# Relation masks made in memory under the attentions, negated scores, weights relative to the first head, ten row buffers

## The reference, cut to what matters

```python
sub, obj = rel_pair_index[:, 0], rel_pair_index[:, 1]          # 10000 pairs, below 1500
att = (q[sub] * k[obj]).sum(-1) / sqrt(64)                     # for each of 8 heads
scores = zeros((8, n, n)).at[:, sub, obj].set(att)
scores = where(adj == 0, -inf, scores)
scores[:, i, i] = 1e-7
out = x + (softmax(scores, axis=2).sum(axis=0) / 8) @ h
```

## Time and profile before

| | |
|---|---|
| median of 3 runs | 4285.27 us (4284.05 to 4287.05) |
| span of the profiled execution | 4283.1 us, 2.2 below the median |
| VectorE busy | 3536.2 us, 83% |
| TensorE busy | 3570.2 us, 83% |
| ScalarE busy | 2616.4 us, 61% |
| POOL busy | 1413.4 us, 33% |
| granted clock of TensorE, mean | 0.912 |

### The profile page before, as it was taken

How to read it: one execution, slowest core, us unless ns; L and a number is a source line. 1 busy time by engine, 2 the same in 40 slices (tenths; PEclk the granted TensorE clock), 3 DMA queues, 4 the chain that set the end, 5 groups by cost and what they waited for, 6 DMA issues and landing times. The chain is left out here.

```text
span 4283.1 us, 55860 instructions
## 1 busy us (share of the span) xinstructions
PE 3570.2 (83%) x20136; PEld 2068.0 (48%) x20136; DVE 3536.2 (83%) x5848; ACT 2616.4 (61%) x3072; POOL 1413.4 (33%) x1417
## 2 busy tenths in 40 slices
PE   6889989879888838687887889899997967788887
PEld 3689989534344414333343344577773422333333
DVE  4699999679999996799999925799984169999996
ACT  3677777559888875588897823454543344444442
POOL 0343200017778794399988811000001100000000
PEclk9999999989998969899898899999998988888888
DMA  4611100211110100511101034000002111111110
GB/s 151 246 32 27 32 27 22 84 46 50 43 45 23 37 17 23 170 40 42 30 20 42 18 125 151 22 19 19 19 9 74 69 64 59 44 49 45 45 44 15
DMA packets 160244, 228.80 MB, mean 53 GB/s; under 512 B 85137, under 2 KB 96288, under 8 KB 154672
## 3 DMA queue, kind: packets, MB, share of 16 engines
q1 hardware_dynamic: 148592, 191.33, 13.8%
q0 software_dynamic: 11376, 33.76, 2.2%
HBM read 158.48 MB, written 66.47 MB: 53 GB/s over the span
## 5 line engine op out<-in xcount | busy, mean ns | idle before, releaser
L1695 DVE SCALAR_TENSOR_TENSOR junk<-expd,mid 128x2048 bf16<-128x2048 f32 x440 | 1036.4, 2356 | 13.8
L579 ACT ACTIVATE steepz<-s1b,thr_h 128x1024 bf16<-128x1024 f32 (+1 forms) x832 | 733.5, 942 | 394.1 <-DVE mask L646 380.9
L732 PE MATMUL acc<-V,mask 128*128 128x198 bf16 (+1 forms) x5504 | 745.8, 274 | 100.4 <-DVE mask L646 51.5
L1595 ACT ACTIVATE junk_s<-expd,nmid 128x2048 bf16<-128x2048 f32 x264 | 528.8, 2003 | 129.6 <-POOL nmid L1655 116.1
L732 PEld LDWEIGHTS acc<-V,mask 128*128 128x128 bf16 x5504 | 478.7, 99 | 163.7 <-DVE mask L646 56.5
L1598 ACT ACTIVATE junk_s<-expd,nmid 128x2048 bf16<-128x2048 f32 x264 | 528.0, 2000 | 0.0
L2140 PE MATMUL psS<-KT,qs 64*128 64x512 f32 x1024 | 367.5, 728 | 130.7 <-DVE m L2253 125.5
L646 DVE TENSOR_TENSOR mask<-steepz,adjT 128x1024 bf16<-128x1024 bf16 (+1 forms) x832 | 438.4, 565 | 18.5 <-ACT steepz L579 8.6
L739 PE MATMUL acc<-V,adjT 128*128 128x99 bf16 (+1 forms) x5504 | 452.5, 220 | 0.0
L739 PEld LDWEIGHTS acc<-V,adjT 128*128 128x128 bf16 x5504 | 368.7, 99 | 49.6 <-issue 1.0
L1467 PE MATMUL psX<-parts,block 128*128 128x512 bf16 x1536 | 364.6, 394 | 10.4 <-DMA block<-adj_dram 10.4
(11 more groups left out here) (306 smaller groups left out, 5941.0 us busy)
## 6 DMA issues: line engine op xcount, KB each, us to landing
rows<-in_adj_dram SPq DMA_DIRECT2D x32, 1024.0 KB, 5.3
s1b<-sT_dram SPq DMA_DIRECT2D x32, 512.0 KB, 3.8
block<-adj_dram SPq DMA_DIRECT2D x32, 512.0 KB, 4.5
adj_dram<-adjT POOLq DMA_DIRECT2D x4, 2048.0 KB, 20.8
rel_table<-zeros POOLq DMA_DIRECT2D x64, 128.0 KB, 19.9
y_dram<-yo SPq DMA_DIRECT2D x32, 256.0 KB, 2.0
step_dram<-xo SPq DMA_DIRECT2D x32, 256.0 KB, 2.0
A<-step_dram SPq DMA_DIRECT2D x8, 1024.0 KB, 13.6
```

What stands on the lines that cost most here:

```text
L579: act.activation(steepz[:, m % RELUS, :], s1b[:, q % 4, :], ACT.Relu, bias=thr_h[:, u, 1, j:j + 1], scale=STEEP).then_inc(relu_ready, 1)
L732: mm = pe.matmul(acc[:, c % 2, i // TB, o:o + 2 * W], mask[:, j % RING, tile(i)], V[:, u, j, 0:2, :].rearrange("p s w -> p (s w)"), start= ...
L1595: act.activation(junk_s[:, 0, :], expd[:, slot[i], :], ACT.Relu, bias=col(nmid, i), accum_out=col(above, i)).then_inc(sums_ready, 1)
L1695: link(dve.scalar_tensor_tensor(junk[:, :], e, col(mid, i), e, ALU.is_gt, ALU.mult, accum_out=col(mass, i)))
```

## The change: what it does

1. In project_stage POOL writes the cast rows of adj to a new table in memory, `plain`, and the cast of tile t waits until the write of t-2 has read its buffer.
2. In the first attention POOL, behind the four writes of adjT, clears the diagonal of `plain`, fills a second table `veil` with 1e30, gathers `plain` at the 10000 pairs (80 indirect DMAs, two in flight), turns a one into 0 and a zero into 1e30, and scatters that into `veil` (80 indirect DMAs, one by one). In the second attention it scatters zeros into `plain` at the pairs.
3. The relation stage loads rows of `veil` and `plain` (as `edge`), both bf16, by SP; the cast, the masks and offdiag are gone.
4. q is scaled by a negative number: the peaks take a minimum, ScalarE's exp has the scale -1 and the minimum as bias, the negation is gone. Peaks are not waited for at once.
5. Weights are relative to head 0: attn starts as edge times a factor plus G of head 0, in one instruction; the diagonal's part is added to attn in its 128x128 block (`diagonal`), and finish is one instruction.
6. Ten row buffers in turn instead of eight, and on VectorE weights and the first two weighings come after the peaks of the first pair; finish in the second pair.

The core of the diff (left out beside declarations: relation_table's code, which veil_table and plain_table replace):

```diff
@@ project_stage @@
+                    for t in range(NT):
+                        pool.wait_ge(cast, t + 1)
+                        pool.dma_start(self.plain.rearrange("(i j) o -> i (j o)", j=N)[tile(t), :],
+                                       rows16[:, t % 2, :]).then_inc(rows_out[t % 2], 16)
...
                         if t >= 2:
                             act.wait_ge(a_ready, 2 * (t - 1))
+                            act.wait_ge(rows_out[t % 2], 16 * (t // 2))
@@ attention_stage, POOL @@
-                    self.relation_table(pool, rel_bufs, rel_sems)
+                    self.veil_table(pool, R, rel_pairs, rel_index, rel_fill, rel_mark, rel_sems, gathered)
                     pool.wait_ge(parked, 64)
+                else:
+                    self.plain_table(pool, R, rel_pairs, rel_index, rel_mark, rel_sems)
@@ mlp_stage @@
-            scale = (D // self.REL_HEADS) ** -0.5
+            scale = -(D // self.REL_HEADS) ** -0.5
@@ veil_table @@
+        pool.dma_start(self.plain[::N + 1, :].rearrange("(p t) o -> p (t o)", p=P), mark[:, 0:NT],
+                       allow_slow_non_contiguous=True).then_inc(sems["in"], 16)
...
+        for b in range(rows.shape[0]):
+            pool.dma_start(rows[b], fill[:, :]).then_inc(sems["cleared"], 16)
+        pool.wait_ge(sems["in"], 32)
+        for c in range(C):
+            if c >= 2:
+                pool.wait_ge(gathered[c % 2], 16 * (c // 2))
+            pool.indirect_dma_start(out=mark[0:R, c:c + 1], out_offset=None, in_=self.plain,
+                                    in_offset=bass.IndirectOffsetOnAxis(ap=index[0:R, c:c + 1], axis=0)
+                                    ).then_inc(gathered[c % 2], 16)
...
+        pool.tensor_scalar(mark[0:R, :], mark[0:R, :], -1.0, -BIG, ALU.add, ALU.mult).then_inc(ready, 1)
...
         for c in range(C):
+            pool.indirect_dma_start(out=self.veil, out_offset=bass.IndirectOffsetOnAxis(ap=index[0:R, c:c + 1], axis=0),
+                                    in_=mark[0:R, c:c + 1], in_offset=None).then_inc(sems["marked"], 16)
             pool.wait_ge(sems["marked"], 16 * (c + 1))
@@ relation_stage, SP @@
+                        if t >= 2:
+                            sp.wait_ge(scores_read, 2 * H * (t - 1))
+                        sp.dma_start(veil[:, t % 2, :], veil_rows[tile(t), :]).then_inc(veil_in[t % 2], 16)
+                        if t >= 2:
+                            sp.wait_ge(weighed, (H + 1) * (t - 2) + 1)
+                        sp.dma_start(edge[:, t % 2, :], plain_rows[tile(t), :]).then_inc(edge_in[t % 2], 16)
@@ relation_stage, VectorE @@
-                    link(dve.scalar_tensor_tensor(y[:, :], nat[:, t, :], own[:, t:t + 1], psO[:, :],
-                                                  ALU.mult, ALU.add))
...
-                    dve.tensor_tensor(xo[:, u, :], y[:, :], xt[:, u, :], ALU.add).then_inc(xo_ready, 1)
+                    dve.scalar_tensor_tensor(xo[:, u, :], psO[:, :], fin[:, t:t + 1], xt[:, u, :],
+                                             ALU.mult, ALU.add).then_inc(xo_ready, 1)
...
                         dve.wait_ge(scores_ready, n + 1)
+                        if half == 1:
+                            dve.wait_ge(scores_read, unit(t, m, 0, b) + 1)
+                        elif t * H + h >= SLOTS:
+                            before = t * H + h - SLOTS
+                            dve.wait_ge(weighed, (H + 1) * (before // H) + before % H + 1)
                         dve.tensor_tensor_reduce(
...
-                        dve.wait_ge(scores_read, n + 1)
-                        if half == 1:
-                            dve.tensor_scalar(nm[:, u, h:h + 1], m1[:, u, h:h + 1], -1.0, None,
-                                              ALU.mult).then_inc(nm_ready, 1)
...
                     link(dve.reciprocal(rz[:, :], z[:, :]))
+                    dve.tensor_scalar(fin[:, t:t + 1], rz[:, 0:1], 1.0 / H, None, ALU.mult)
+                    link(dve.tensor_scalar(r[:, :], rz[:, :], z[:, 0:1], None, ALU.mult))
+                    link(dve.tensor_tensor_reduce(wj[:, :], e0[:, :], r[:, :], 1.0, 0.0, ALU.mult, ALU.add, om[:, t:t + 1]))
+                    link(dve.tensor_tensor_reduce(wj[:, :], ed[:, :], r[:, :], 1.0, 0.0, ALU.mult, ALU.add, own[:, t:t + 1]))
...
+                    w = attn[:, t % 2, :]
+                    if h == 0:
+                        ins = dve.scalar_tensor_tensor(w, edge[:, t % 2, :], om[:, t:t + 1], G(t, 0), ALU.mult, ALU.add)
+                    else:
+                        dve.wait_ge(weighed, (H + 1) * t + h)
+                        ins = dve.scalar_tensor_tensor(w, G(t, h), r[:, h:h + 1], w, ALU.mult, ALU.add)
+                    ins.then_inc(weighed, 1)
+
+                def diagonal(t):
+                    d = attn[:, t % 2, tile(t)]
+                    dve.wait_ge(weighed, (H + 1) * t + H)
+                    dve.scalar_tensor_tensor(d, self.ident[:, :], own[:, t:t + 1], d, ALU.mult, ALU.add).then_inc(weighed, 1)
+                    dve.wait_ge(weighed, (H + 1) * (t + 1))
...
                 for t in range(NT + 1):
-                    if t >= 1:
-                        weights(t - 1)
-                        weigh(t - 1, 0)
-                        weigh(t - 1, 1)
                     for m in range(PAIRS):
                         for half in range(2):
                             if t < NT:
                                 peaks(t, m, half)
-                            if t >= 1 and m < PAIRS - 1:
-                                weigh(t - 1, 2 * m + 2 + half)
-                            if t >= 3 and m == 0 and half == 1:
+                            if t >= 1 and m >= 1:
+                                weigh(t - 1, 2 * m + half)
+                            if t >= 3 and m == 1 and half == 0:
                                 finish(t - 3)
-                    if t + 1 < NT:
-                        masks(t + 1)
+                        if t >= 1 and m == 0:
+                            weights(t - 1)
+                            weigh(t - 1, 0)
+                            weigh(t - 1, 1)
+                    if t >= 1:
+                        diagonal(t - 1)
```

More of the change, by code:

```diff
@@ L329, in project_stage @@
                 id_done = self.sem(st, "id_done")
+                rows_out = [self.sem(st, f"rows_out{u}") for u in range(2)]
             block = st.enter_context(nc.Block())
@@ L2016, in top_p_stage, with pair_index @@
         self.top_p_step(1, natA, trB, xa_dram, xT_dram, kq_dram, parts_dram, y_dram)
-    def relation_table(self, pool, bufs, sems):
-        pairs_dram = self.a["L3_gnn_rel_pair_index"]
-        E = pairs_dram.shape[0]
-        R = next(r for r in range(P, 0, -1) if E % r == 0)
-        C = E // R
-        table = self.table
-        zeros, pairs, index, ones = bufs
-        ready = sems["ready"]
-        pool.dma_start(pairs[0:R, :, :], pairs_dram.rearrange("(r c) o -> r c o", r=R)).then_inc(sems["in"], 16)
-        pool.memset(ones[:, :], 1.0).then_inc(ready, 1)
-        pool.memset(zeros[:, :], 0.0).then_inc(ready, 1)
-        pool.wait_ge(ready, 2)
-        width = zeros.shape[1]
-        rows = table.rearrange("(b p w) o -> b p (w o)", p=P, w=width)
-        for b in range(rows.shape[0]):
-            pool.dma_start(rows[b], zeros[:, :]).then_inc(sems["cleared"], 16)
+    def pair_index(self, pool, R, pairs, index, sems):
+        ready = sems["ready"]
+        pool.dma_start(pairs[0:R, :, :], self.a["L3_gnn_rel_pair_index"].rearrange("(r c) o -> r c o", r=R)
+                       ).then_inc(sems["in"], 16)
@@ L2044, in relation_table, with plain_table @@
             pool.wait_ge(sems["marked"], 16 * (c + 1))
-    def relation_stage(self, nat, Bflat, KT, qT_dram, table, x_dram, out):
+    def plain_table(self, pool, R, pairs, index, mark, sems):
+        C = self.a["L3_gnn_rel_pair_index"].shape[0] // R
+        self.pair_index(pool, R, pairs, index, sems)
+        pool.memset(mark[:, :], 0.0).then_inc(sems["ready"], 1)
+        pool.wait_ge(sems["ready"], 3)
+        for c in range(C):
+            pool.indirect_dma_start(out=self.plain, out_offset=bass.IndirectOffsetOnAxis(ap=index[0:R, c:c + 1], axis=0),
+                                    in_=mark[0:R, c:c + 1], in_offset=None).then_inc(sems["marked"], 16)
+            pool.wait_ge(sems["marked"], 16 * (c + 1))
@@ L2223, in _ @@
                 link = chain(dve, dve_done)
-                def masks(t):
-                    u = t % 2
-                    dve.wait_ge(rows_cast, t + 1)
-                    dve.wait_ge(rel_in[u], 16 * (t // 2 + 1))
-                    link(dve.tensor_tensor(edge[:, u, tile(t)], edge[:, u, tile(t)], offdiag[:, :], ALU.mult))
-                    link(dve.tensor_tensor(rel[:, u, :], edge[:, u, :], rel[:, u, :], ALU.mult))
-                    link(dve.tensor_scalar(veil[:, :], rel[:, u, :], -1.0, BIG, ALU.add, ALU.mult))
```

(12 more changed lines are left out.)

146 lines of the change are left out of this document (69 added, 77 removed).

## The result

| kernel | median, us | lowest to highest | ratio to before, 95% interval |
|---|---|---|---|
| before | 4285.26 | 4284.05 to 4287.05 | 1 |
| after | 4241.97 | 4235.11 to 4247.73 | 0.9898 [0.9884, 0.9912] |

The change gains 43 us where 116 were forecast, and 4242 lies above the range of 4148 to 4212. The profiled span is 4233.3 us, 49.8 less than before (4283.1). These 49.8 divide at three marks. The relation stage's first load of q is issued at 3458.10 where it was at 3454.72: the stages ahead take 3.4 us more. From there to the first peak are 6.6 us where 11.3 were: -4.8. From the first peak to the end are 768.64 us where 817.06 were: -48.4, and here 113.3 had been forecast (the stage's 118.1 less the 4.8).

A forecast was written before the change was run, and what follows sets the result against it. VectorE's work in the relation stage's sixteen row tiles was taken to bound the kernel. The stage's -118.1 us and +2 ahead of it gave -116 from 4285.3, so 4169 us; range 4148 to 4212.

The forecast's parts named there:

- Work of VectorE per tile: Relation stage: 7.46 us removed and 0.45 added per row tile, net 7.0, leaving 40.8 us of VectorE work.
- Does TensorE keep up?: Relation stage: whether TensorE delivers scores in time; VectorE's waiting stays 1.6 us per tile, bounds 0.5 and 5.
- Rival 2: Relation stage: TensorE stays longer at 1.2 GHz, 2.9 us more per tile, +44, 4213 us; chance 0.16.
- 1.6 of waiting per tile kept: Relation stage: VectorE's wait for scores stays as before, 1.6 us per tile, with a similar, slightly milder disturbance.
- The old wait of 5.41 on TensorE: Relation stage: TensorE's idle stretch during weights and two weighings, 5.41 us before, becomes 4 to 4.5.
- Start and tail: Relation stage's ends: first peak 4.8 us earlier without cast and masks; tail behind the last tile 8.4 us shorter.
- Row writes: Project stage: POOL's writes of cast rows fit narrowly beside the loads, +1 us, bounds 0 and 30.
- rival 3: Project stage: the row writes hold ScalarE's casts, +2 us per tile, 4199 us; chance 0.05.
- POOL's chain: First attention: POOL's fills, gathers and scatters end between 611 and 786 us, taken as 670, hidden behind VectorE's work.
- rival 4: First attention: slow POOL gathers delay its end; gain gone at 5 us a gather, 4370 us at 6; chance 0.05.
- The stages ahead: Stages before the relation stage: +1 us for row writes and +1 for contention in both attentions, +2 together.
- rival 1: Relation stage: removed VectorE waits were free, so 22.7 us of the gain vanish, 4192 us; chance 0.14.

The follow-up runs named there:

- the first experiment: The changed kernel with finish(t-3) moved back from the second pair to the first, behind its peaks and ahead of weights; 4174.57 us, ratio 0.9738.
- e9: The changed kernel with finish back in the first pair, with tables of 2 columns of pairs instead of 80, so 2 gathers and 2 scatters; 4167.80 us, ratio 0.9735.

## Why the prediction was wrong, point by point

- **Work of VectorE per tile: right in kind, somewhat too high.** 40.8 forecast, 39.7 measured (the period of 47.7 less 8.0 of waiting). The rest of 1.1 is mostly the sixteen peaks: 0.05 each for a removed wait was too low, it is 0.12. The fused weighing of head 0 is 2.35 as taken; weights take 1.44 (3760.93 to 3762.37) where 1.44 plus 0.15 was expected; the diagonal 0.35, with what follows 0.39, for 0.30.
- **The step that failed: the place of finish, in "Does TensorE keep up?".** That part kept 1.6 us of waiting a tile, with bounds of 0.5 and 5, and costed the move of finish to the second pair at nothing. The prediction followed VectorE's order for what weights and weighings do to TensorE, and asked of finish only its own duration, 1.40 to 0.67. It didn't ask who waits for finish: TensorE's first apply step, through the one psO, with VectorE's next scores queued behind. The runs showed 6.75 us of waiting a tile in its place, 67 us in the whole. The wait was already in the trace of before, 2.78 us. Rival 2 named the right symptom (a period over 44 with waits for psS) and a wrong mechanism; its 2.9 us a tile would have been 4213, and undoing the move alone gives back 67 us of the 73 missing.
- **1.6 of waiting per tile kept: wrong in this kernel, and too low in the first experiment.** Measured were 8.0 (6.75, 1.07 and 0.17). With finish early the period is 42.7 against 42.4 forecast, the first peak to the end 702.5 against 703.8. That nearness is partly luck: the waiting is 3.0 us there, 1.4 more than forecast, and the work 1.1 less, and the two errors nearly cancel.
- **The old wait of 5.41 on TensorE** was expected to become 4 to 4.5 idle with the same disturbance: 3.8 in the first experiment, with the slow step behind it, as expected. It could be avoided: one weighing fewer ahead of the second pair's peaks, and one buffer more, take 22 to 24 us off.
- **Start and tail: right.** -4.8 at the start, as forecast. Tail: the last pair of peaks ends at 4182.22, the span 51.1 us later. In before it ended 58.0 later; of the 8.4 forecast, 2.6 (the weighing and the diagonal that cover the last exp) are no saving behind that point, so 52 were expected.
- **Row writes, +1 forecast (rival 3: +30): wrong in size.** The project stage is 2.8 us longer in after, 5.7 on average over the runs (156.8 against 151.1): the 5.4 and 6.1 us of two single transfers became 7.4 for a write beside row loads, which themselves land in 7.1 where they took 5.8 in this stage before (medians of 16). Two casts that were 4.4 us apart in before are 6.7 apart in after (80.28 to 87.00).
- **POOL's chain (rival 4): hidden, as forecast.** Gathers 1.9 us apart, last scatter at 650.0 where 670 was taken and 611 to 786 were the bounds. Their contention was put at 1; the profiles of the first attention speak for some 5, with a cause that isn't shown.
- **The stages ahead, +2 forecast: too low.** The first load of q is issued at 3454.7 and 3455.7 us in the two kernels of the old form, and at 3457.2 to 3467.8 (mean 3463.1) in the twelve of the new: 8 us on average. In after it was 3.4, in the first experiment 11.3; this is why that run is 5.6 above the forecast of 4169 though its relation stage is 1.3 shorter than forecast.
- **Waits free (rival 1): refuted** by the run with the waits put back, +25 us.

## What to carry to other kernels

When an instruction is moved, its own duration is the smaller question. Write down who waits for its result, and what stands behind that waiter in the waiter's queue; a wait that only guards a single buffer (psO here) holds all independent work queued behind it. Where one engine paces another, spread long instructions so that the paced one never stands idle for several us: the last 22 to 24 us came from one weighing less in the long stretch, for the price of one buffer. A wait that is short in the trace (2.78 us for finish) is worth following before its cause is moved. And when work is taken off an engine, look for waits that it had covered (the masks had covered 3.2 us of waiting for the last exp).

## What the runs showed of the hardware

- A wait on the instruction just before costs VectorE 0.12 us behind a peak with its accumulator read, and as much behind a 2.35 us weighing; 22 of them in a tile were worth 25 us of 4175 in the whole kernel.
- POOL's gathers of 125 two-byte elements, two in flight, start 1.9 us apart; scatters, each waited for, 3.4 us apart, of which 1.3 is issue, as before.
- The stretch from the first attention to the relation stage, the same code in all kernels of the new form but e9 (fewer scatters), differed by up to 10 us between single profiles (2674 to 2684). Differences of a few us in one stage were only to be seen by timing marks in the traces, and even there not beyond doubt.
